# Queries and keys of the second attention as scaled pairs of 16-bit halves

## What is computed

```
q = (x @ Wq.T).reshape(B, T, H, Dh)      # H = 16 heads, Dh = 128, T = 2048
k = (x @ Wk.T).reshape(B, T, H, Dh)
v = (x @ Wv.T).reshape(B, T, H, Dh)
q = _apply_rope(q, cos, sin)
k = _apply_rope(k, cos, sin)
scores = jnp.einsum('bthd,bshd->bhts', q, k) * scale      # scale = Dh ** -0.5
scores = jnp.where(causal[None, None], scores, -jnp.inf)
attn = jax.nn.softmax(scores, axis=-1)
y = jnp.einsum('bhts,bshd->bthd', attn, v).reshape(B, T, H * Dh)
return y / 3.0 @ Wo.T
```

## Time and profile before

| | |
|---|---|
| median of 3 runs | 1728.66 us (1725.97 to 1731.49) |
| profiled execution, its own time | 1724.86 us |
| its span, first to last instruction | 1723.1 us |
| mean granted TensorE clock | 0.99 |
| TensorE busy, whole span | 1648.0 us, 96% |
| VectorE busy | 1373.5 us, 80% |
| ScalarE busy | 1238.2 us, 72% |
| GpSimd busy | 1081.6 us, 63% |

### The profile page before, as it was taken

One profiled execution on the slowest core, in us unless ns is written; L12 is line 12 of the kernel. 1 busy time (PEld: TensorE's weight loads), 2 busy tenths in 40 slices (PEclk: granted clock), 3 DMA queues, 4 the chain that ended last, 5 costly groups with the idle time before them and its releaser, 6 DMA issues.

```text
span 1723.1 us, 37269 instructions
## 1 busy us (share of the span) xinstructions
PE 1648.0 (96%) x11566; PEld 1418.2 (82%) x11566; DVE 1373.5 (80%) x3611; ACT 1238.2 (72%) x3255; POOL 1081.6 (63%) x1098
## 2 busy tenths in 40 slices
PE   6998998989979999999999999999999999999899
PEld 4777886778868888888888888888888888887787
DVE  7458856375588998999899999999899899997553
ACT  4335652344449889888898988988988889888642
POOL 2534112644427777887886886886877688687732
PEclk9999999999989999999999999999999999999999
DMA  8843037760027896795887987877789678687500
GB/s 294 244 99 50 2 106 240 166 157 12 1 48 128 134 159 120 133 168 108 147 143 123 147 140 126 146 134 146 125 136 166 112 140 155 110 147 136 115 22 28
DMA packets 636133, 215.96 MB, mean 125 GB/s; under 512 B 587296, under 2 KB 622752, under 8 KB 635808
## 3 DMA queue, kind: packets, MB, share of 16 engines
q1 hardware_dynamic: 625568, 200.71, 59.5%
q0 software_dynamic: 10368, 12.85, 4.5%
HBM read 51.06 MB, written 19.80 MB: 41 GB/s over the span
## 4 chain that ended last, share of the span: by engine, by line
PE 83%; DVE 8%; ACT 3%; issue 3%; DMA 2%; POOL 1%; SPq 0%; ACTq 0%; POOLq 0%; DVEq 0%
PE phase_scores L1277 22%; PE phase_y L166 9%; PE phase_y L167 9%; PE phase_y L168 9%; PE phase_ring L166 5%; PE phase_ring L168 5%; PE phase_ring L167 5%; PE phase_banks L777 2%; PE phase_up_ps L166 2%; PE phase_up_ps L168 2%; PE phase_up_ps L167 2%; PE phase_banks L796 2%; PE phase_banks L166 1%; PE phase_banks L168 1%; PE phase_banks L167 1%
## 5 line engine op out<-in xcount | busy, mean ns | idle before, releaser
L2330 POOL TENSOR_TENSOR phase_split<-phase_p,phase_split 128x512 f16<-128x512 f32 (+3 forms) x640 | 650.8, 1017 | 180.7 <-ACT phase_split L2299 142.4
L1311 ACT ACTIVATE phase_p<-phase_scores,phase_bias 128x512 f32<-128x512 f32 (+3 forms) x680 | 420.9, 627 | 83.2 <-DVE phase_bias L2325 60.9
L2299 ACT ACTIVATE phase_split<-phase_p 128x512 f16<-128x512 f32 (+3 forms) x640 | 345.5, 577 | 0.0
L166 PE MATMUL phase_y<-phase_pt,phase_v_hi 128*128 128x256 f16 (+1 forms) x1152 | 310.7, 271 | 2.1 <-DMA phase_pt<-phase_split 2.1
L167 PE MATMUL phase_y<-phase_pt,phase_v_hi 128*128 128x256 f16 (+1 forms) x1152 | 307.7, 267 | 0.0
L1290 DVE TENSOR_REDUCE phase_peaks<-phase_scores 128x1 f32<-128x512 f32 (+1 forms) x408 | 266.6, 669 | 48.9 <-PE phase_scores L1277 45.1
L168 PE MATMUL phase_y<-phase_pt,phase_v_lo 128*128 128x256 f16 (+1 forms) x1152 | 302.7, 267 | 0.0
L1277 PE MATMUL phase_scores<-phase_k_hi,phase_q_hi 128*128 128x512 f32 (+3 forms) x640 | 258.1, 403 | 8.7 <-ACT phase_p L1311 6.5
L1277 PE MATMUL phase_scores<-phase_k_hi,phase_q_lo 128*128 128x512 f32 (+3 forms) x640 | 232.3, 363 | 0.0
L1277 PE MATMUL phase_scores<-phase_k_lo,phase_q_hi 128*128 128x512 f32 (+3 forms) x640 | 231.6, 362 | 0.0
L2699 POOL TENSOR_TENSOR sb_x<-sb_x,phase_part 128x512 f32<-128x512 f32 x128 | 164.6, 1286 | 65.3 <-ACT phase_part L2556 57.1
(11 more groups left out here) (313 smaller groups left out, 4480.1 us busy)
## 6 DMA issues: line engine op xcount, KB each, us to landing
phase_pt<-phase_split SPq DMA_TRANSPOSE x640, 3.2
y_rows<-phase_zero SPq DMA_DIRECT2D x16, 512.0 KB, 7.5
phase_e_up<-expert_up SPq DMA_DIRECT2D x16, 352.0 KB, 4.2
phase_e_dn<-expert_down SPq DMA_DIRECT2D x16, 256.0 KB, 5.6
xn_rows<-phase_ln_xn SPq DMA_DIRECT2D x8, 512.0 KB, 2.9
sb_x<-y_rows POOLq DMA_DIRECT2D x8, 512.0 KB, 6.4
late_raw_qk<-qk SPq DMA_DIRECT2D x16, 256.0 KB, 3.2
phase_logits_t<-expert_up SPq DMA_DIRECT2D x8, 352.0 KB, 4.1
```

Of the source, the lines that this page charges most:

```text
L166: pe.matmul(out, left_hi[c], r_hi, start=first and c == 0, stop=False)
L1311: act.activation(self.p_room(act, key)[:, 0:width], self.scores[:, at:at + width], ACT.Exp, bias=self.bias[:, t % 2:t % 2 + 1], accum_out= ...
L2299: act.activation(hi, value, ACT.Copy).then_inc(*self.t_hi.one)
L2330: pool.tensor_tensor(lo, value, hi, ALU.subtract).then_inc(*self.t_lo.one)
```

## The change

Queries and keys are stored as 16-bit halves (`near_hi`, `near_lo`, float16), two bytes an element, with a factor. The matmuls of the scores are as many and as wide as before.

- The factor `qk_scale` comes from the sum of squares of the head's rounded query and key weights. Five new small steps a head, of three new kinds: `qk_norm(h)` on ScalarE squares 128x512 elements and adds them up; `qk_bound(h)` adds across partitions on TensorE into a ring bank, scales on VectorE and takes the power on GpSimd; `qk_steep(h)` on VectorE makes the factors for the exponential in three instructions, each waiting for the one before.
- The factor is put in where queries and keys leave the ring bank, and divided out by the exponential, which takes a scale of its own (`steep`); the maximum's bias is multiplied by `fall` in place of -1. The multiplication of the query weights by Dh ** -0.5 is gone, in `act_weights` and in `Gated.act_next`.
- `finish` is one instruction of 128x512 on ScalarE and one on VectorE, in place of two of 128x256 on each, with queries and keys at two places of one room.
- `finish` waits for the factor. The first `qk_steep` of a head's successor waits until the exponentials two heads back are done, and the first bias of a head waits for `qk_steep`.
- `load_qk(h)` waits until the squares of head h - 1 are taken. Six small signals are one, `factors`.
- `TABLE`, `LEAD` and `PLACES` are new for every engine.

```diff
@@ Gated.act_next
-        act.activation(core.raw_qk[:, :, 0, :], core.raw_qk[:, :, 0, :], ACT.Copy, scale=float(DH) ** -0.5).then_inc(*self.next_scaled.one)
-        act.wait_ge(*self.next_scaled[self.then])
         act.activation(core.qk_hi[:], core.raw_qk[:], ACT.Copy).then_inc(*self.next_hi["qk"].one)
@@ LEAD
-    "pe": {"S": 0, "s": -27, "p": 3, "v": 0, "o": -3, "b": 1},
+    "pe": {"S": 8, "s": -2, "p": 4, "v": 1, "o": -2, "b": 1, "B": 1},
@@ Attention1
-    RING = ("project", "values", "bound", "next_flip")
+    RING = ("project", "values", "bound", "qk_bound", "next_flip")
...
-        self.k_hi, self.k_lo = (sb(n, [P, T], F32R) for n in ("k_hi", "k_lo"))
-        self.q_hi, self.q_lo = (sb(n, [P, 2, 2 * P], F32R) for n in ("q_hi", "q_lo"))
+        self.near_hi, self.near_lo = (sb(n, [P, 17 * 2 * P], F16) for n in ("near_hi", "near_lo"))
@@ dve_peak
-        dve.tensor_scalar(self.bias[:, t % 2:t % 2 + 1], self.top[:, t % 2:t % 2 + 1], -1.0, self.SHARE, ALU.mult, ALU.add).then_inc(*self.biased.one)
+        if t == 0:
+            dve.wait_ge(*self.factors["steep", h, 2])
+        dve.tensor_scalar(self.bias[:, t % 2:t % 2 + 1], self.top[:, t % 2:t % 2 + 1], self.fall[:, h % 2:h % 2 + 1], self.SHARE,
+                          ALU.mult, ALU.add).then_inc(*self.biased.one)
+
+    def act_exp_of_chunk(self, act, key):
...
+                       scale=self.steep[:, h % 2:h % 2 + 1], accum_out=self.sums[:, t % 2, c:c + 1]).then_inc(*self.p_done.one)
@@ pe
+            elif what == "qk_bound":
+                h, = key
+                pe.wait_ge(*self.qk_squared[key])
...
+                self.pe_ring_wait(pe, step)
+                pe.matmul(self.ring_bank(step)[:, 0:1], self.ones[:], self.qk_power[:, h % 2:h % 2 + 1], start=True, stop=True).then_inc(*self.qk_bounded.one)
@@ act
-                act.activation(self.q_hi[:, cur, :], both[:, 0, :], ACT.Copy)
-                act.activation(self.k_hi[:, where], both[:, 1, :], ACT.Copy).then_inc(*self.qk_hi_done.one)
+                act.wait_ge(*self.qk_scaled[h,])
+                act.activation(self.near(self.near_hi, g), both, ACT.Copy, scale=self.qk_scale[:, h % 2:h % 2 + 1]).then_inc(*self.qk_hi_done.one)
+            elif what == "qk_norm":
...
+                act.activation(self.core.squares[:], as_f32(self.qk_hi[:].rearrange("p k a b -> p (k a b)")), ACT.Square,
+                               accum_out=self.qk_power[:, h % 2:h % 2 + 1]).then_inc(*self.qk_squared.one)
@@ dve
-                dve.tensor_tensor(self.q_lo[:, g % 2, :], both[:, 0, :], as_f32(self.q_hi[:, g % 2, :]), ALU.subtract)
-                dve.tensor_tensor(self.k_lo[:, where], both[:, 1, :], as_f32(self.k_hi[:, where]), ALU.subtract).then_inc(*self.qk_done.one)
+                dve.scalar_tensor_tensor(self.near(self.near_lo, g), self.both(("project", h, g)), self.qk_scale[:, h % 2:h % 2 + 1],
+                                         self.near(self.near_hi, g), ALU.mult, ALU.subtract).then_inc(*self.qk_done.one)
...
+            elif what == "qk_steep":
...
+                dve.tensor_scalar(steep, scale, scale, -float(DH) ** 0.5, ALU.mult, ALU.mult).then_inc(*self.factors.one)
+                dve.wait_ge(*self.factors["steep", h, 0])
+                dve.reciprocal(fall, steep).then_inc(*self.factors.one)
+                dve.wait_ge(*self.factors["steep", h, 1])
+                dve.tensor_scalar(steep, fall, -1.0, None, ALU.mult).then_inc(*self.factors.one)
@@ pool
+            if what == "qk_bound":
...
+                pool.tensor_tensor(self.qk_scale[:, now], self.qk_bound[:, now], self.core.half[:, 0:1], ALU.pow).then_inc(*self.qk_scaled.one)
```

145 lines of the change are left out of this document (96 added, 49 removed), and 8 rows, old and new, of the table LEAD.

## The result

| | before | changed |
|---|---|---|
| median, measured side by side (5 runs each) | 1731.46 us (1725.97 to 1733.29) | 1748.14 us (1744.7 to 1749.3) |
| profiled execution, its own time | 1724.86 us | 1748.14 us |
| its span | 1723.1 us | 1746.4 us |
| mean length of a pass (two heads) | 138.95 us | 141.0 us |

The changed kernel is slower: 1.0108 times the time before, 95% interval 1.0091 to 1.0125. The forecast was 1705 us, a gain of 1.4%; the range ended at 1723. It was wrong in sign.

The account below looks back on a forecast made before the run. TensorE was taken to bound 1072 us of the second attention. Terms of -28.7 (matmuls), +1.3 (start) and +3.9 (waits) gave -23.5 us, so 1701.4 on the profiled execution, 1705 as median; range 1697 to 1723 us.

Parts of the forecast that it names:

- Part 1: Score matmuls on TensorE: 16-bit steps of 0.2155 us instead of 0.2317 for 512 columns, plus joints; 32.9 us saved.
- the type saves nothing: Rival on the score matmuls: float32's slower step has another cause than type; 1.6 us gained, 1727 us, chance 0.06.
- Part 2: Added TensorE work, one qk_bound a head: 2.2 us, leaving 30.7, of which 28.7 us counts.
- Part 3: VectorE's finish, small steps and bias: +0.6 us a pass (-0.1 to +2.9); lost waiting room costs 3.9 us in all.
- 2 or 3: Sign of the forecast: VectorE's waits for TensorE fall from 6.4 us a pass to this many.
- Part 4: ScalarE, GpSimd and transfers: ScalarE gets some 0.8 us a pass on top of 122.8; neither engine sets the pace.
- If ScalarE's slack of 12 us were gone, the same work would cost 6 us: Side estimate for ScalarE's added work in the second attention: 6 us only without slack, otherwise no cost.
- Part 5: Start of the stage: VectorE idles for GpSimd's power before the first rope; +1.3 us (0 to +4).
- VectorE becomes a second bound: Rival: VectorE keeps 3 to 5 us of waits a pass; some 13 us gained, 1715 us, chance 0.26.
- Slower: the waits stay: Rival: VectorE keeps all 6.4 us of waits a pass, plus finish's waits for its factor; 1750 us, chance 0.08.
- if TensorE waits more than 2 us a pass: Condition stated beforehand, on TensorE's waits in a pass, under which the prediction counts as wrong.
- the last one: Condition for being wrong: the 1580 to 1622 us stretch, left unchanged in the forecast, moves by more than 4 us.

Follow-up runs that it names:

- e4: Kernel before with one edit: queries and keys stored as 16-bit halves, no factor, old tables and waits; 1701.80 us, ratio 0.9855.
- e3: Changed kernel with constants for both the exponential's scale and the bias's factor, not read from memory; factor's steps and waits kept; 1724.83 us, ratio 0.9985.
- e7: Changed kernel without its factor, its steps and waits; constants in exponential and bias, new tables; 1709.57 us, ratio 0.9934.
- e1: Changed kernel with the exponential's scale as a constant in the instruction instead of read from memory; 1726.82 us, ratio 0.9998.
- e6: e4 with one edit: the exponential reads a scale of 1.0 from memory; old order, no factor; 1715.56 us, ratio 0.9973.
- e10: Kernel before (float32 pairs, old order) with the exponential reading a scale of 1.0 from memory; 1730.18 us, ratio 1.0048.
- e11: e4 with the rounding of the probabilities, not the exponential, reading scale 1.0 and bias 0.0 from memory; 1742.50 us, ratio 1.0131.
- e5: e4 with the changed kernel's new tables, less the letters of the factor's steps; 1711.98 us, ratio 0.9955.
- e9: e7 with the tables of the kernel before: 16-bit halves, merged finish, no factor, old order; 1692.86 us, ratio 0.9834.

## Why the prediction was wrong, point by point

The forecast missed by 43 us, 1705 against 1748. Three pieces make nearly all of it: the exponential's scale from memory, 19 us, which no term had; the new order, 17 us, which no term had beyond the start; and the factor's steps and waits, 9 us, for which parts 2 and 3 had some 6 us together. The matmuls, part 1, were right.

**Part 1, the matmuls.** Right. Without `qk_bound`, which e4 doesn't have, the forecast's terms make 32.9 x 0.935 = 30.8 us, less 3.9 for waits 26.9; e4 gained 25. The step was 0.2150 us in the row above and 0.2168 in the mean of 580 of them in e4 (0.2155 taken, 0.2133 to 0.2175 as ends). The rival that the type saves nothing is out. Of the page that speaks for it, "TensorE: Matmul & The Clock Gate" of the Trainium skill, section "Back-to-back issue gap", the formula gives an estimate of 215.8 ns for 512 columns. It agrees with the 16-bit matmuls here (215.0) and not with the float32 ones (231.7).

**Part 2**, `qk_bound` on TensorE: its 2.2 us were not measured alone. The part has no wait in it, and in the changed kernel from 520 to 1570 us TensorE waits 2.6 us ahead of `qk_bound`, half of it for the squares of ScalarE.

**Part 3, VectorE.** The work was sized too low. Its groups in the changed kernel, 520 to 1580 us, beside the earlier trace rows:

```profile
L2669 DVE SCALAR_TENSOR_TENSOR phase_near_lo<-phase_ring,phase_qk_scale,phase_near_hi 128x512 f16<-128x512 f32 x120 | 89.2, 743 | 7.1 <-ACT phase_near_hi L2558 6.2
...
L2692 DVE TENSOR_SCALAR phase_steep<-phase_qk_scale 128x1 f32<-128x1 f32 x15 | 3.1, 204 | 0.0
L2694 DVE RECIPROCAL phase_fall<-phase_steep 128x1 f32<-128x1 f32 x15 | 2.5, 164 | 0.5
L2696 DVE TENSOR_SCALAR phase_steep<-phase_fall 128x1 f32<-128x1 f32 x15 | 2.3, 154 | 0.5
L2683 DVE TENSOR_SCALAR phase_qk_bound<-phase_ring 128x1 f32<-128x1 f32 x15 | 2.3, 153 | 0.0
```

743, 204, 164, 154 and 153 ns are the forecast's 740 and 157 but for one, which reads two operands from memory (with one, in e3, it takes 153); the bias is the term that was mis-sized, 60 ns in place of 0 to 30. Counted from start to start without waits, VectorE needed 132.5 us a pass before and 135.8 now: 3.3 us more, where +0.6 was forecast and +2.9 was the upper end. In e4 it is 131.4. Its waits for TensorE, forecast at "2 or 3" us a pass, are (25.2 + 5.6) / 7.45 = 4.1; the 5.6 us stand in the row of the masked chunks, and 7.45 is the number of passes in 1050 us. How much of the 9 us between e7 and e3 is VectorE's was not tried.

**Part 4, ScalarE. This is the step that failed.** It counted what instructions ScalarE loses and gets, "some 0.8 us a pass", and ended with "Neither sets the pace". It did not look at the instructions that stay. The diff shows the line of the exponential with `scale=self.steep[...]`, and the prediction mentions it in no term: 80 instructions a pass, 7.3 us by their starts and 8.5 by their durations, are ten times the change that was counted. Everything else that the change does to ScalarE takes about 1 us a pass off it: 123.8 us of work before and 122.8 in e1, where the exponential's scale is a constant again. The prediction looked at the same question for VectorE's bias, 32 a pass, and not for ScalarE's 80. A page of the Trainium skill has the price: "ScalarE: Activation LUTs", section "What ACT_TABLE_LOAD costs", says that each per-partition operand from memory adds about 93 ns. The traces agree: by the starts 91 to 93 ns for one on the exponential and 185 for two on the rounding, by the durations 95 to 112 and 195. It would have given an estimate of 7.4 us a pass.

**Part 4, "If ScalarE's slack of 12 us were gone, the same work would cost 6 us".** The second error is in the picture, and the price alone would not have cured it: 122.8 + 7.3 is still 130 of 135 us. An engine was taken to cost nothing until it is full. e6, e10 and e11 show otherwise: ScalarE never fills, and each microsecond of its work costs 0.4 and 0.5 us of pass with the 16-bit matmuls and 0.2 with the float32 ones. A reason that fits, though no run tests it: scores, maximum, bias, exponential and the free bank go round through three engines with four banks, and with VectorE at 131 and ScalarE at 123 of 135 us there is little slack in any place of that ring.

**Part 5, the start.** Forecast: the rope some 3 us later after the first statistics. GpSimd's memset and VectorE at the stage's start in the changed kernel, beside the earlier trace rows:

```profile
480.85 0.20 POOL L2725 MEMSET phase_ones<- 128x128 f32 x1 [6.31 <-DVE sb_x L2036]
480.89 1.41 DVE L241 BATCH_NORM_STATS2 phase_ln_stats<-sb_x 128x6 f32<-128x256 f32 x4
...
484.25 0.16 DVE L281 TENSOR_TENSOR phase_ln_tmp<-phase_ln_rstd 128x4 f32<-128x4 f32 x1 [1.50 <-POOL phase_ln_rstd L260]
...
486.00 0.68 DVE L2660 TENSOR_TENSOR phase_crossed<-phase_ring,late_rope 32x512 f32<-32x512 f32 x1
```

The statistics in the kernel before:

```profile
476.46 1.41 DVE L241 BATCH_NORM_STATS2 phase_ln_stats<-sb_x 128x6 f32<-128x256 f32 x4
```

The rope starts 486.00 - 480.89 = 5.11 us after the statistics, before 478.68 - 476.46 = 2.22: 2.9 later, with 1.50 us of waiting for GpSimd where 1.3 were forecast. Right. That the whole stage begins 4.4 us later in this execution than in that of before (the memset then started at 476.42) is not the change's: among the fourteen profiled executions, with the same work ahead but for one instruction, it began between 470.1 and 480.9 us.

**Order.** The sum has no term for the tables beyond the start: "all lists are new" stands under a rival only. e4 and e5 put 17 us on it, as much as on the operand. In e9 against e7 it is 17 us again. A term like this can't be read from the trace before; it should have widened the range.

**The rivals.** "VectorE becomes a second bound" (1715 us) describes e5 and e7 (0.9955 and 0.9934, 1721 and 1717 on the base of 1728.7), where a pass is 137.3 to 137.9 us, but its cause, VectorE's waits, is only a part. "Slower: the waits stay" gave 1750 us at a chance of 0.08, and 1748 came out, for another reason: with VectorE's work complete and the exponential's scale constant, e1 has a pass of 138.65 us, not 139.6, and only breaks even. What made it slower than before was ScalarE's operand, and that rival leaves ScalarE's work as it was; the number was near by luck. The condition named as proof of error, "if TensorE waits more than 2 us a pass", was met: 31.8 / 7.45 = 4.3 for the exponentials alone. So was the last one: from 1580 to 1622 us VectorE has 32.72 us of work in place of 22.84 and ScalarE 36.43 in place of 27.19, because the stage there is not yet in its end.

## What to carry to other kernels

Where a diff turns a constant into an operand from memory, multiply its price by the count of that instruction, on every engine, before anything that is added or removed; look in the trace for two instructions of the same shape and source that differ in just that. An engine at 90% among engines that free each other's banks is not a free engine: here each microsecond of work cost 0.2 to 0.5 us of pass, before the engine was full. When a change has a gain and a cost in separable parts, run the gain alone: the plainest edit here (four lines, e4) was faster than the kernel that was built around it.

## What the runs showed of the hardware

- A ScalarE instruction with a scale from memory is about 105 ns longer, almost whatever its width (exponential of 512 columns 691 to 797 ns, of 256 columns 478 to 590, of 128 columns 368 to 463); with scale and bias 195 ns (rounding, 645 to 840). The next instruction starts 91 to 93 ns later for one operand (512 columns 571 to 662 ns, 384 columns 463 to 555, 256 columns 356 to 448) and 185 for two (520 to 705). On VectorE one operand makes a 128x1 instruction 60 ns longer (154 to 214).
- A float32r matmul of 512 columns starts 0.2317 us after the last, a 16-bit one 0.2150, both at a granted clock of 1.00, the 2.4 GHz level.
- Instructions that were not edited have longer durations in the fuller schedules: the rounding of 512 columns 641 ns before and 660 in the changed kernel and in e6, the exponential 691 before and 708 in e11. By the starts nothing grew: 520 or 521 ns from the rounding to the next instruction in all of them, 569 to 571 for the exponential. To size ScalarE's work, compare starts.
